# Moving an exchange between two groups of moves, and three pieces of work between VectorE, ScalarE and GpSimd, in a fused attention and spiking feed-forward layer

## What is computed

```
h    = norm(xn) * ln_scale + ln_bias
c_q  = h @ w_down_q.T ; c_kv = h @ w_down_kv.T             # 64 latents each
q, k, v = c_q @ w_up_q.T, c_kv @ w_up_k.T, c_kv @ w_up_v.T # 16 heads of 64
q, k = rope(q), rope(k)                                    # all 64 dimensions
attn = softmax(q k^T / 8) v  @ w_out.T + xn
y    = relu(xn @ W_fc.T)^2 @ W_proj.T                      # 512 hidden values
ffn  = (spikes of 5 steps of a leaky integrator driven by y) / 5
```

## Time and profile before

| | |
|---|---|
| median of 3 runs | 1167.56 us (1165.77 to 1170.44) |
| the profiled execution, its own time | 1171.33 us |
| its span (first to last instruction) | 1169.3 us |
| mean granted clock of TensorE | 0.985 of full speed |
| instructions | 25819 |
| time for one batch in the middle (two batches in 68.51 us) | 34.26 us |

### The profile page before, as it was taken

One profiled execution on the slowest core, in us unless ns is written; L12 is line 12 of the kernel. 1 busy time (PEld: TensorE's weight loads), 2 busy tenths in 40 slices (PEclk: granted clock), 3 DMA queues, 4 the chain that ended last, 5 costly groups with the idle time before them and its releaser, 6 DMA issues.

```text
span 1169.3 us, 25819 instructions
## 1 busy us (share of the span) xinstructions
PE 1057.1 (90%) x6880; PEld 712.1 (61%) x6880; DVE 985.0 (84%) x1350; ACT 845.5 (72%) x2945; POOL 808.3 (69%) x837
## 2 busy tenths in 40 slices
PE   3788999999999999999999999999999999999976
PEld 2555666666666666666666666666666666666643
DVE  3878888899888889988889898888998888888851
ACT  3777777777777777777877777777777777777640
POOL 4677678667667876766876777686776778666720
PEclk9989999999999999999999999999999999989997
DMA  5377777877777787776777777777777777866761
GB/s 168 110 188 199 196 195 187 220 190 185 199 193 186 193 223 187 184 206 175 186 208 200 189 190 201 191 186 215 193 186 195 198 188 191 222 172 176 195 157 32
DMA packets 93280, 217.95 MB, mean 186 GB/s; under 512 B 22464, under 2 KB 43200, under 8 KB 93120
## 3 DMA queue, kind: packets, MB, share of 16 engines
q1 hardware_dynamic: 93248, 217.57, 70.1%
HBM read 7.77 MB, written 4.19 MB: 10 GB/s over the span
## 4 chain that ended last, share of the span: by engine, by line
PE 45%; issue 19%; DVE 16%; POOL 13%; SPq 3%; ACT 2%; DMA 1%; DVEq 1%; POOLq 0%; ACTq 0%
PE ps_s L315 12%; PE ps_u L329 11%; POOL partner L728 5%; POOL qk L731 5%; PE ps_qk L305 5%; DVE turned L600 5%; PE ps_b L406 4%; PE ps_a L368 4%; DVE qk L586 3%; PE ps_qk L306 3%; SPq L247 2%; PE ps_a L381 2%; DVE u_n L614 2%; DVE count L647 2%; ACT raw L494 2%
## 5 line engine op out<-in xcount | busy, mean ns | idle before, releaser
L482 ACT ACTIVATE prob<-ps_s,neg_max 128x256 f32<-128x256 f32 x1024 | 473.1, 478 | 165.3 <-DVE neg_max L591 162.4
L728 POOL TENSOR_TENSOR partner<-partner,rope_sb 128x512 f32<-128x512 f32 x256 | 327.3, 1279 | 269.8 <-DMA partner<-raw 269.6
L591 DVE TENSOR_REDUCE neg_max<-ps_s 128x4 f32<-128x1024 f32 x256 | 309.9, 1210 | 92.3 <-PE ps_s L315 89.7
L731 POOL TENSOR_TENSOR qk<-qk,partner 128x512 f32<-128x512 f32 x256 | 325.9, 1273 | 20.1
L315 PE MATMUL ps_s<-qk 64*128 64x256 f32 x2048 | 294.4, 406 | 49.8 <-POOL qk L731 48.6
L600 DVE STREAM_TRANSPOSE turned<-prob 128x1024 f32<-128x1024 f32 x256 | 315.5, 1232 | 1.2 <-issue 0.2
L329 PE MATMUL ps_u<-gathered,ckv 128*64 128x256 f32 x2048 | 279.3, 394 | 9.5 <-DMA gathered<-turned 9.5
L315 PEld LDWEIGHTS ps_s<-qk 64*128 64x128 f32 x2048 | 178.5, 188 | 161.5 <-issue 82.8
L494 ACT COPY raw<-ps_qk 128x512 f32<-128x512 f32 x256 | 152.7, 597 | 98.4 <-PE ps_qk L306 94.7
L482 ACT ACTIVATION_READ_ACCUMULATOR prob<-ps_s,neg_max 128x1 f32 x1024 | 213.3, 208 | 0.0
L586 DVE TENSOR_TENSOR qk<-ps_qk,rope_sb 128x512 f32<-128x512 f32 x256 | 175.2, 684 | 37.2 <-ACT raw L494 31.2
(11 more groups left out here) (57 smaller groups left out, 859.3 us busy)
## 6 DMA issues: line engine op xcount, KB each, us to landing
gathered<-turned SPq DMA_DIRECT2D x1024, 128.0 KB, 2.3
partner<-raw SPq DMA_DIRECT2D x256, 256.0 KB, 2.4
x_sb<-in_x SPq DMA_DIRECT2D x32, 128.0 KB, 2.3
resid<-early SPq DMA_DIRECT2D x32, 128.0 KB, 2.0
out<-out_sb SPq DMA_DIRECT2D x32, 128.0 KB, 2.1
turned<-in_wup SPq DMA_DIRECT2D x2, 512.0 KB, 5.5
rope_sb<-in_rope SPq DMA_DIRECT2D x1, 512.0 KB, 6.5
turned<-in_wo_t SPq DMA_DIRECT2D x1, 512.0 KB, 7.9
```

Of the source, the lines that this page charges most:

```text
L482: last = nc.scalar.activation(prob[:, s % 2, :, h, :, t, :].rearrange("p j k c -> p k j c"), ps_s[:, s % 2, h, t, :].rearrange("p (k j c) ...
L591: nc.vector.tensor_reduce(neg_max[:, s % 2, :, :], ps_s[:, s % 2, :, :, :], AXIS_X, ALU.max, negate=True).then_inc(max_ready, 1)
L728: nc.gpsimd.tensor_tensor(other, other, sin_sb, ALU.mult).then_inc(sin_ready, 1)
L731: nc.gpsimd.tensor_tensor(qk[:, s % 4, :, :], qk[:, s % 4, :, :], other, ALU.add).then_inc(rope_done, 1)
```

## The change

Five edits:
- SyncE: the first part of a group's moves has 4 DMAs instead of 8, the second part 12; the exchange stays between them.
- VectorE: in p = 7 `add_spikes` comes ahead of `rotate`; `normalise_u` is gone.
- ScalarE: a new `copy_spread` copies each broadcast of reciprocals from `ps_b` to `spread` (two halves), in p = 0 to 3 ahead of `copy_u`. A new `square` squares the relu's output in p = 6, 7, behind `copy_u`.
- GpSimd: `normalise_u` multiplies the latents in place by `spread`, in p = 1, 2, 4, 5. `square` is gone, and `residual` moves from p = 4 to p = 6.
- Buffers: `u_sb` has two halves, one per batch, in place of `u_raw` and `u_n`. `copy_u` waits for the output product of two batches ago. TensorE's broadcast waits for `copy_spread`, and `attention_out` for GpSimd's `normalise_u`, chunk by chunk.

```diff
-        u_raw = sb("u_raw", [P, PAIRS, S])
-        u_n = sb("u_n", [P, PAIRS, S])
+        u_sb = sb("u_sb", [P, 2, PAIRS, S])
+        spread = sb("spread", [P, 2, 2, S])
...
# SyncE, step
-                    move(g + turn, s + turn, (0, 1))
+                    move(g + turn, s + turn, (0,))
                 if (s + LEAD["project"]) % 2 == 1 and not outside(g + LEAD["project"], STEPS):
                     exchange(g + LEAD["project"], s + LEAD["project"])
                 if (s + turn) % GROUP == 0 and not outside(g + turn - 1, STEPS):
-                    move(g + turn - 1, s + turn - 1, (2, 3))
+                    move(g + turn - 1, s + turn - 1, (1, 2, 3))
...
# TensorE, broadcast_rden and attention_out
                 if c > 0:
-                    pe.wait_ge(u_norm, done(CHUNKS * b + c - 1))
+                    pe.wait_ge(bc_evac, done(CHUNKS * b + c - 1))
...
-            def attention_out(b, c):
+            def attention_out(b, c, par):
                 if c == 0:
-                    pe.wait_ge(u_norm, done(CHUNKS * b + CHUNKS - 1))
+                    pe.wait_ge(bc_evac, done(CHUNKS * b + CHUNKS - 1))
+                pe.wait_ge(u_norm, done(CHUNKS * b + c))
...
# ScalarE
-                if pair % 2 == 0 and not outside(b - 1, B):
-                    act.wait_ge(u_norm, done(CHUNKS * (b - 1) + pair // 2))
-                nc.scalar.copy(u_raw[:, pair, :], ps_u[:, 0:S]).then_inc(u_evac, 1)
+                if pair % 2 == 0 and not outside(b - 2, B):
+                    act.wait_ge(out_part, done(CHUNKS * (b - 2) + pair // 2))
+                nc.scalar.copy(u_sb[:, (s // PAIRS) % 2, pair, :], ps_u[:, 0:S]).then_inc(u_evac, 1)
+
+            def copy_spread(b, c):
+                act.wait_ge(bc_ready, done(CHUNKS * b + c))
+                act.wait_ge(u_norm, done(CHUNKS * b + c - 2))
+                nc.scalar.copy(spread[:, c % 2, :, :], ps_b[:, :].rearrange("p (j s) -> p j s", j=2)).then_inc(bc_evac, 1)
+
+            def square(n, half):
+                act.wait_ge(relu_done, done(2 * n + half))
+                c = slice(2 * half, 2 * half + 2)
+                nc.scalar.activation(relu_sb[:, c, :], relu_sb[:, c, :], ACT.Square).then_inc(sq_done, 1)
...
+                if p < 4 and not outside(b - 1, B):
+                    copy_spread(b - 1, p)
                 if not outside(g, STEPS):
                     copy_u(g, s, i)
+                if p in (6, 7) and not outside(b + 1, B):
+                    square(b + 1, p - 6)
...
# VectorE, step (the function normalise_u is gone)
+                if p == 7 and not outside(b - 1, B):
+                    add_spikes(b - 1, 1 - b0)
                 if not outside(g + LEAD["project"], STEPS):
                     rotate(g + LEAD["project"], s + LEAD["project"])
-                if p == 7 and not outside(b - 1, B):
-                    add_spikes(b - 1, 1 - b0)
-                if p < 4 and not outside(b - 1, B):
-                    normalise_u(b - 1, p)
...
# GpSimd (the function square is gone)
+            def normalise_u(b, c, par):
+                pool.wait_ge(bc_evac, done(CHUNKS * b + c))
+                pool.sem_inc(pool_waited, 1)
+                pool.wait_ge(u_evac, done(PAIRS * b + 2 * c + 1))
+                two = u_sb[:, par, 2 * c:2 * c + 2, :]
+                nc.gpsimd.tensor_tensor(two, two, spread[:, c % 2, :, :], ALU.mult).then_inc(u_norm, 1)
...
-                if p == 4 and not outside(b + 2, B):
+                if p in (1, 2, 4, 5) and not outside(b - 1, B):
+                    normalise_u(b - 1, {1: 0, 2: 1, 4: 2, 5: 3}[p], 1 - b0)
+                if p == 6 and not outside(b + 2, B):
                     residual(b + 2, b0, i + 1)
-                if p in (6, 7) and not outside(b + 1, B):
-                    square(b + 1, p - 6)
```

More of the change, by code:

```diff
@@ L158, in build @@
         rt_ready, rt_evac = sem("rt_ready"), sem("rt_evac")
-        bc_ready, u_norm = sem("bc_ready"), sem("u_norm")
+        bc_ready, bc_evac, u_norm = sem("bc_ready"), sem("bc_evac"), sem("u_norm")
         out_part = sem("out_part")
@@ L184, in build @@
             "dve": [cos_ready, max_ready, turn_done, rden_ready, stats_ready, moments_ready,
-                    latent_split, lif, u_norm, acc_ready, final_done],
+                    latent_split, lif, acc_ready, final_done],
             "act": [u_evac, raw_ready, exp_done, tr_evac, ckv_ready, relu_done, rt_evac,
-                    xn_ready, z_ready, latent_hi],
-            "pool": [sin_ready, rope_done, eps_ready, rstd_ready, shift_ready, sq_done, res_ready,
+                    xn_ready, z_ready, latent_hi, bc_evac, sq_done],
+            "pool": [sin_ready, rope_done, eps_ready, rstd_ready, shift_ready, u_norm, res_ready,
                      rden_hi, rden_split],
@@ L400, in broadcast_rden @@
                 last.then_inc(bc_ready, 1)
-            def attention_out(b, c):
+            def attention_out(b, c, par):
                 if c == 0:
-                    pe.wait_ge(u_norm, done(CHUNKS * b + CHUNKS - 1))
+                    pe.wait_ge(bc_evac, done(CHUNKS * b + CHUNKS - 1))
+                pe.wait_ge(u_norm, done(CHUNKS * b + c))
                 for pair in (2 * c, 2 * c + 1):
-                    last = nc.tensor.matmul(ps_b[:, 0:S], wvo_sb[:, pair, :], u_n[:, pair, :],
+                    last = nc.tensor.matmul(ps_b[:, 0:S], wvo_sb[:, pair, :], u_sb[:, par, pair, :],
                                             start=(pair == 0), stop=(pair == PAIRS - 1))
@@ L429, in extras @@
                 if not outside(b - 1, B) and p >= 4:
-                    attention_out(b - 1, p - 4)
+                    attention_out(b - 1, p - 4, 1 - b0)
                 if p == 0:
@@ L607, in invert_sums @@
                 nc.vector.reciprocal(rden[:, :, :], den[:, b0, :, :]).then_inc(rden_ready, 1)
[L609 to L615, removed]
             def moments_of(n, par, i):
```

## The result

The changed kernel takes 1122.93 us (median of 4 runs, 1121.14 to 1125.72); the kernel before took 1166.66 us (4 runs, 1164.34 to 1170.44). The ratio is 0.9604, with a 95% interval of 0.9572 to 0.9636. Forecast: 1124 us, range 1103 to 1153. The profiled execution took 1125.72 us, with a span of 1123.8.

A forecast was written before the change was run, and what follows sets the result against it. VectorE and the exchange were taken to bound p1 to p5, TensorE the rest. Step terms sum to -1.38 us a batch, -41.4 over 30 batches, -2 for the stretches outside: 1124 us, range 1103 to 1153.

The forecast's parts named there:

- p1: Second of a batch's eight steps: ScalarE's new copy ahead of copy_u delays TensorE's weighing, +0.50 us a batch.
- p7: Last of a batch's eight steps: spike sum ahead of the rotation lets TensorE's transposes start earlier, -0.34 us a batch.
- p3: Fourth of a batch's eight steps: the wait of the next scores for GpSimd goes, -1.30 us a batch.
- p4: Fifth of a batch's eight steps: its output product waits for ScalarE's fourth copy, +0.27 us a batch.
- p5: Sixth of a batch's eight steps: the feed-forward product no longer waits for VectorE's count, -0.39 us a batch.
- The exchange behind four moves: SyncE's queue: GpSimd has the exchange's data 3.3 us sooner, ending the p4 scores' wait; booked as -1.30 in p3.
- The squares: ScalarE, end of p = 6 and p7: 0.6 us each, costing nothing while below about 1 us.
- The stretches ahead and behind: Parts of the run outside the 30 full batches: they have the exchange's wait too, given -2 us.
- Slower by the function table: Rival: Square forces ScalarE table loads, 1220 us; chance 0.10, shared with a GpSimd product ahead of an urgent rope.
- Late moves: Rival: the twelve moves behind the exchange land late, p4's weighing waits some 0.7 us a batch; 1145 us, chance 0.18.
- TensorE alone: Rival: TensorE alone sets the pace, copies covered in p1 and p4; -2.15 us a batch, 1101 us, chance 0.10.
- nothing gained: Rival: GpSimd's 28.1 us and the waits between its parts come to the old period; 1166 us, chance 0.06.

The follow-up runs named there:

- Experiment 4: The changed kernel with the spike sum behind the rotation again: 1129.31 us, ratio 0.9643 to the kernel before.
- Experiments 6 and 9: 6: changed kernel, ScalarE's two latent copies moved into p1, 0.9601; 9: kernel 8 with third and fourth spread copies ahead of the exponentials, 0.9514.
- experiment 1: The kernel before with only the new split of the moves (4 ahead of the exchange, 12 behind): 1163.61 us, ratio 0.9936.
- experiment 2: The changed kernel with the old split of the moves (8 ahead of the exchange, 8 behind): 1147.45 us, ratio 0.9799.
- experiment 5: The changed kernel with the squares on GpSimd again, behind the residual: 1122.34 us, ratio 0.9597.
- kernel 8: The changed kernel with VectorE's transpose of p = 0 ahead of its rotation: ratio 0.9579.
- kernels 11 and 12: 11: changed kernel, latent copies in p1, spread copies 2 to 4 before exponentials, 0.9578; 12: also early p = 0 transpose, by-token latent copy back, 0.943.

## Why the prediction was right

**The sum.** For the batch shown, against the same steps before, which need four more rows of the kernel before (p1, p2, p7 and the p0 behind it):

```profile
613.67 1.14 PE L315 MATMUL ps_s<-qk 64*128 64x256 f32 x8
...
616.66 1.13 PE L315 MATMUL ps_s<-qk 64*128 64x256 f32 x8
...
638.97 1.14 PE L315 MATMUL ps_s<-qk 64*128 64x256 f32 x8
...
644.10 1.13 PE L315 MATMUL ps_s<-qk 64*128 64x256 f32 x8
```

| step | forecast | measured in the batch shown | mean of two batches |
|---|---|---|---|
| p1 | +0.50 | 596.91 - 593.28 = 3.63, +0.64 | +0.53 |
| p2 | -0.12 | 600.75 - 596.91 = 3.84, -0.24 | -0.21 |
| p3 | -1.30 | 604.60 - 600.75 = 3.85, -1.34 | -1.30 |
| p4 | +0.27 | 608.55 - 604.60 = 3.95, +0.34 | +0.34 |
| p5 | -0.39 | 613.02 - 608.55 = 4.47, -0.49 | -0.54 |
| p7 | -0.34 | 622.43 - 617.49 = 4.94, -0.19 | -0.19 |

The batch shown comes to -1.28, the mean of two batches to -1.36, for a forecast of -1.38. Every step and sign was right, and the mechanism too, but for what waits first in p1 (below); that the total is right to 0.02 is in part luck, since p5 gave 0.15 more than booked and p7 0.15 less. One reading of the first part is off without harm: by its own rows TensorE stops in three of the eight steps, so five run without a wait, not six. The walk of VectorE held to 0.1 us: its row maximum of p4 starts at 606.41, 17.0 us behind the batch's first scores; the forecast was 626.8 - 609.81 = 17.0.

```profile
606.41 1.21 DVE L606 TENSOR_REDUCE neg_max<-ps_s 128x4 f32<-128x1024 f32 x1
...
620.36 0.42 DVE L662 SCALAR_TENSOR_TENSOR acc_t<-count,ps_b 128x256 f32<-128x256 f32 x1 [0.46 <-PE ps_b L407]
```

Here is also what p7 lost. The spike sum (620.36) waited 0.46 us and began 0.21 us behind the modelled end of its product (619.13 + 1.02), where the forecast allowed 0.06. Experiment 4 gives the order's price: 0.20 us a batch, some 6 us (4.6 by the ratios), of the 10 us booked.

**ScalarE's copy in p1 and p4.** Right in step and sign. Every second batch differs in p1: it takes 3.63 us in the batch shown and 629.70 - 626.30 = 3.40 in the next, so the 0.64 is the longer of two and the mean is 0.53 for 0.50. p4 grew by 0.34 for 0.27. In p1 the first to wait is not the weighing, as forecast, but the broadcast ahead of it, which needs the bank (595.46). Experiments 6 and 9 show that both waits are a matter of order.

**The exchange behind four moves.** The step booked 1.30 us for p3. The step got that much shorter, but it isn't what the edit is worth. Alone it brings a regular batch nothing (experiment 1), and beside the rest 0.69 us a batch (experiment 2). Alone, the split gives 0.6% and the normalising with its buffers 1.6%; the changed kernel gives 4.0%, of which the spike order is 0.4. So the two are worth more together than apart, which the first part of the prediction stated ("lifting one of the two alone would leave the other") and its sum by steps could not.

**The squares.** Correct as "cost nothing" (0.678 us each, forecast 0.6), and they gained nothing either (experiment 5). GpSimd's product takes 1.276 us, forecast 1.28.

**The number of batches.** This part was partly luck. The profiled executions are 45.5 us apart, for a forecast of 43.4. Between the row maxima that open the third and the twenty-ninth batch on VectorE, the kernel before takes 129.84 to 1022.10, the changed one 129.96 to 985.48: 36.7 us for 26 batches, where 26 times 1.38 makes 35.9. Of these, 1.6 come from one batch of before (506.66 to 542.55, 35.89 us) in which TensorE's granted clock was 0.50 of full speed, the lower of its two levels, for some 3 us.

The stretches ahead and behind should have given the other 7.5 and gave 8.8, but not as forecast. The one ahead gave nothing: in one of its batches the issue of 12 moves took 8.81 us instead of 7.54, and TensorE waited 2.0 us for them. Kernel 5 has the usual 7.54 there, kernel 8 has 8.39 without a wait, and kernels 11 and 12 show it again (9.00 and 8.70); why is open. The one behind gave 8.9, some 3.6 of them because the batch of before that starts at 1022.10 took 37.88 us. There the granted clock was 0.50 from 1038 to 1042, right behind a long wait:

```profile
1038.18 2.08 PE L315 MATMUL ps_s<-qk 64*128 64x256 f32 x8 [2.49 <-POOL qk L731]
```

In the other long batch too the clock fell behind a wait for GpSimd that was longer than usual (1.75 us; the one in the earlier trace rows is 1.27). In the changed kernel, without that wait, none of the 26 batches takes over 32.95 us. The two batches are together some 5 us longer than regular ones, and the forecast had no term for them.

**The rivals.** *Slower by the function table*: excluded, `ACT_TABLE_LOAD` x1 with Square in use. The Trainium skill, "ScalarE: Activation LUTs", section "Table sets", does not name Square among the cheap functions that are in every table set; in this kernel it lives with Exp on one load. *Late moves*: nearly false for the changed kernel (16.4 us of weight loads' waiting, 19 times; 13.5 us, 12 times before), and close behind it: in the batches shown TensorE waits 0.95 us for the moves in kernel 1 and 0.61 in kernel 11. *TensorE alone* and *nothing gained*: neither; TensorE still waits in p1, p4 and p7.

**What stays open.** Why the spike sum starts 0.2 us behind its product while row maxima start 0.05 behind theirs was not tried. Nor is it known why p1 takes 3.63 and 3.40 us in turn in the changed kernel. The split with the transpose of p0 ahead of the normalising, on the kernel before, was not run either.

## What to carry to other kernels

Where an engine with a wait and an engine without gaps stand side by side, the wait's length is not the gain: ask of each edit alone what ends last without the others, and expect the sum of single gains to fall short of the joint one (here 0.6% and 1.6% against 3.6%). Copies that an engine makes for others belong into its own waits (here between the projection's copy and the exponentials), not ahead of the copy that the bound engine needs. A queue of small transfers can be a bound like an engine: here 12 moves take 7.54 us to issue in nearly every batch, so their end moves with their start, and the transpose in front of them is what to bring forward. And read more than one batch: here neighbouring ones differ by up to 0.23 us in a step.

## What was not expected of the hardware

The recorded duration of an exponential depends on what runs in front of it. It is 0.47 us after a wait for the row maximum, and 0.51 for the whole group of four when the first starts 0.47 us behind the start of a copy of 0.62 us. The distance from start to start within the group is 0.45 to 0.46 us in both cases, so nothing is lost. A sum over durations overrates ScalarE's load, since neighbours overlap: the window has 28.95 us a batch, and the forecast, from durations, was 29.9.

```profile
595.56 0.62 ACT L495 COPY raw<-ps_qk 128x512 f32<-128x512 f32 x1
596.03 0.51 ACT L483 ACTIVATE prob<-ps_s,neg_max 128x256 f32<-128x256 f32 x1
...
596.49 0.50 ACT L483 ACTIVATE prob<-ps_s,neg_max 128x256 f32<-128x256 f32 x1
...
600.36 0.47 ACT L483 ACTIVATE prob<-ps_s,neg_max 128x256 f32<-128x256 f32 x1 [1.02 <-DVE neg_max L606]
...
600.82 0.47 ACT L483 ACTIVATE prob<-ps_s,neg_max 128x256 f32<-128x256 f32 x1
```
